# Values kept in SBUF for all tokens, query and key parts written in 4 KB rows, and both attention-stage loops written out

## The reference, cut to what matters

```python
x = x + _layernorm(_L0_attn_ref(_layernorm(x), qkv_w, qkv_b, out_w, out_b))
# _L0_attn_ref: 16 heads of width 16
qkv = x @ qkv_w.T + qkv_b
scores = einsum('bhqd,bhkd->bhqk', q, k) / sqrt(16)
out = einsum('bhqk,bhkd->bhqd', softmax(scores), v)
return out @ out_w.T + out_b
```

## Time and profile before

| | us |
|---|---|
| median of 3 runs | 2459.27 |
| lowest, highest | 2456.72, 2468.26 |
| the profiled execution, its own time | 2469.44 |
| its span, first to last instruction | 2467.7 |

### The profile page before, as it was taken

How to read it: one execution, slowest core, us unless ns; L and a number is a source line. 1 busy time by engine, 2 the same in 40 slices (tenths; PEclk the granted TensorE clock), 3 DMA queues, 4 the chain that set the end, 5 groups by cost and what they waited for, 6 DMA issues and landing times. The chain is left out here.

```text
span 2467.7 us, 40737 instructions
## 1 busy us (share of the span) xinstructions
PE 2150.2 (87%) x14580; PEld 1510.8 (61%) x14580; DVE 1582.9 (64%) x2593; ACT 1256.8 (51%) x2510; POOL 667.2 (27%) x483
## 2 busy tenths in 40 slices
PE   7589999989999945885699999999999999588896
PEld 6533333333333314775588888888888888477775
DVE  7478888888888516775354545455454544568876
ACT  3227777777777713443443444344444444355451
POOL 1010000000000003555333343325243434233432
PEclk9859999999999857888699999999999999799998
DMA  7942232222320021112311221303121211200000
GB/s 227 286 103 72 54 96 62 79 72 61 96 62 28 24 89 49 52 42 80 131 52 53 69 63 60 96 28 121 52 70 53 69 53 61 68 26 27 25 25 19
DMA packets 118685, 176.40 MB, mean 71 GB/s; under 512 B 19289, under 2 KB 73697, under 8 KB 114401
## 3 DMA queue, kind: packets, MB, share of 16 engines
q1 hardware_dynamic: 118496, 173.90, 23.6%
HBM read 126.15 MB, written 46.92 MB: 70 GB/s over the span
## 5 line engine op out<-in xcount | busy, mean ns | idle before, releaser
L576 DVE TENSOR_REDUCE att_sb_mx<-att_ps_psM 128x1 f32<-128x1024 f32 x512 | 607.1, 1218 | 122.3 <-PE att_ps_psM L609 119.5
L714 ACT ACTIVATE att_sb_pt<-att_ps_psS 128x512 f32<-128x512 f32 x1024 | 537.1, 603 | 178.7 <-PE att_ps_psS L627 178.6
L609 PE MATMUL att_ps_psM<-stack_sb_k,stack_sb_q 48*128 48x512 f32 x1024 | 413.8, 480 | 26.1 <-PEq L185 22.8
L627 PE MATMUL att_ps_psS<-stack_sb_q,stack_sb_k 50*128 50x512 f32 x1024 | 390.7, 463 | 38.1 <-ACT att_sb_pt L714 23.2
L627 PEld LDWEIGHTS att_ps_psS<-stack_sb_q,stack_sb_k 50*128 50x128 f32 x1024 | 173.2, 191 | 363.5 <-ACT att_sb_pt L714 306.8
L636 PE MATMUL att_ps_psO<-att_sb_pt,stack_sb_v 128*32 128x512 f32 x2048 | 285.3, 630 | 17.1 <-ACT att_sb_osb L707 17.1
L609 PEld LDWEIGHTS att_ps_psM<-stack_sb_k,stack_sb_q 48*128 48x128 f32 x1024 | 175.2, 193 | 54.6 <-issue 24.2
L2329 POOL TENSOR_TENSOR gla_sb_dm<-gla_sb_dm,gla_sb_masked 128x1024 f32<-128x1024 f32 x64 | 159.3, 2510 | 84.8 <-DMA gla_sb_dm<-decay_rows 84.7
L1995 ACT ACTIVATE gla_sb_sg<-gla_ps_psP 128x512 f32<-128x512 f32 x64 | 38.2, 597 | 280.6 <-PE gla_ps_psP L1756 280.6
L2012 ACT ACTIVATE gla_sb_dm<-gla_sb_dm,gla_sb_neg_g 128x128 f32<-128x128 f32 x512 | 156.3, 391 | 5.0 <-POOL gla_sb_dm L2329 5.0
L2211 DVE TENSOR_TENSOR gla_sb_dm<-gla_ps_psA,gla_sb_dm 128x512 f32<-128x512 f32 x128 | 82.2, 684 | 113.1 <-PE gla_ps_psA L1880 112.6
(11 more groups left out here) (251 smaller groups left out, 4952.8 us busy)
## 6 DMA issues: line engine op xcount, KB each, us to landing
gla_sb_dm<-decay_rows SPq DMA_DIRECT2D x32, 1024.0 KB, 5.4
qk_parts<-qkv_sb_part SPq DMA_DIRECT2D x64, 256.0 KB, 4.1
gla_sb_eg<-decay_exp SPq DMA_DIRECT2D x64, 256.0 KB, 6.6
values<-qkv_sb_va SPq DMA_DIRECT2D x32, 256.0 KB, 3.7
stack_sb_q<-qk_parts SPq DMA_DIRECT2D x64, 128.0 KB, 3.4
stack_sb_k<-qk_parts SPq DMA_DIRECT2D x32, 256.0 KB, 4.1
stack_sb_v<-values SPq DMA_DIRECT2D x16, 512.0 KB, 4.3
att_sb_rb<-sums SPq DMA_DIRECT2D x32, 256.0 KB
```

Of the source, the lines that this page charges most:

```text
L576: nc.vector.tensor_reduce(mx[:, qh, 8 * r + c:8 * r + c + 1], psM[:, t % 2, :], AX.X, ALU.max).then_inc(maxima_taken, 1)
L609: mm = pe.matmul(psM[:, t % 2, c * ST:(c + 1) * ST], q[rs, g, qh, j, n * P:(n + 1) * P], k[rs, g, j, c * ST:(c + 1) * ST], start=True, sto ...
L627: pe.matmul(psS[:, ring_slot(pos), :], k[rs, g, j, s * P:(s + 1) * P], q[rs, g, qh, j, :], start=True, stop=True).then_inc(ring_done, 1)
L714: nc.scalar.activation(pt[:, s % (LAG + 2), ORDER[i], :], psS[:, (pos + 1) % 3, :], ACT.Exp, scale=AD ** -0.5).then_inc(ring_taken, 1)
```

## The change

It has five parts. (1) `stacks.v` holds the values of all 32 token tiles, 17 columns per head (a one and 16 values) and 15 zeros after the last head; `va` is a view of it, so DVE writes values where PE reads them, and `values` with its writes and reads is gone. A value product still takes 32 columns as weights: its own 17 and the 15 that follow, which belong to the next head. (2) POOL sets the ones and zeros after the first inverse root, not before it. (3) `qk_parts` has the high and low row of a channel side by side, so that each of the 8 writes moves 64 rows of 4 KB. (4) Keys are loaded in 6 DMAs a block (4 before); the queries' second half of block 0 is loaded in the last super-tile's turn, not in the one before it. (5) All loops of the two phases are written out.

```diff
-        va = m.sb("va", [P, 2, NT, AH, VW])
+        va = stacks.heads
...
+        def over_all(eng, body):
+            for i in range(NST):
+                body(i, i % 2, i == NST - 1)
...
                 if isinstance(i, int) and i == NST - 2:
                     for o in range(2):
                         sp.wait_ge(part_out[o], 16 * 8)
-                        sp.wait_ge(v_out[o], 16 * NG)
                     stacks.load_first(sp, 0, 0, True)
+                if last:
                     stacks.load_second(sp, 0, 0)
...
                     for g in range(2):
-                        sp.dma_start(parts[mt // 2, i, 2 * (mt % 2) + g].rearrange("a c t -> c a t"),
+                        sp.dma_start(parts[mt // 2, i, 2 * (mt % 2) + g],
                                      part[64 * g:64 * g + 64, u, mt, :, :].bitcast(F32)).then_inc(part_out[u], 16)
-                sp.wait_ge(v_taken, 2 * (i + 1))
-                for g in range(NG):
-                    sp.dma_start(v_aug[i, g], va[:, u, :, HG * g:HG * (g + 1), :].rearrange("p n h c -> p n (h c)")
-                                 ).then_inc(v_out[u], 16)
...
-                if pair == 0 and not first(i, 2):
-                    dve.wait_ge(v_out[u], 8 * NG * (i - u))
                 ns = slice(2 * pair, 2 * pair + 2)
-                nc.vector.tensor_tensor(va[:, u, ns, :, 1:AD + 1],
+                nc.vector.tensor_tensor(va[:, NT * i + 2 * pair:NT * i + 2 * pair + 2, :, 1:VC],
...
             minus_half(nc, pool, half, half_set)
-            for u in range(2):
-                nc.gpsimd.memset(va[:, u, :, :, 0:1], 1.0).then_inc(va_set, 1)
-                nc.gpsimd.memset(va[:, u, :, :, AD + 1:VW], 0.0).then_inc(va_set, 1)
             inverse_root(nc, pool, rs, half, ln_step, LN, rs_ready)
             pool.wait_ge(rs_ready, 1)
+            nc.gpsimd.memset(va[:, :, :, 0:1], 1.0).then_inc(va_set, 1)
+            nc.gpsimd.memset(stacks.v[:, :, AH * VC:], 0.0).then_inc(va_set, 1)
+            pool.wait_ge(va_set, 2)
             stacks.minus(nc.gpsimd, 0)
...
-        self.v = m.sb("v", [P, NG, KT, HG * VW])
+        self.v = m.sb("v", [P, TOKENS // P, AH * VC + VW - VC])
+        self.heads = self.v[:, :, 0:AH * VC].rearrange("p n (h c) -> p n h c", c=VC)
...
-        for blk, a, n in runs(K_PART):
-            if fresh and AD * (blk + n) > 32:
+        for blk, a in enumerate(K_PART):
+            if fresh and AD * (blk + 1) > 32:
...
         self.load_queries(sp, b, 1, g, self.second_in[g])
-        sp.dma_start(self.v[:, g, :, :].rearrange("p (s n) c -> p s n c", s=QH),
-                     self.v_aug[b, :, g].rearrange("s p n c -> p s n c")).then_inc(self.second_in[g], 16)
...
         def over_pairs(eng, body):
-            for g in range(NG):
-                body(0, g, False)
-            with eng.Fori(1, BATCH - 1) as b:
+            for b in range(BATCH):
                 for g in range(NG):
-                    body(b, g, False)
-            for g in range(NG):
-                body(BATCH - 1, g, g == NG - 1)
+                    body(b, g, (b, g) == (BATCH - 1, NG - 1))
...
-                    mm = pe.matmul(psO[VW * j:VW * (j + 1), :], v[:, g, s, VW * j:VW * (j + 1)],
+                    h = VC * (HG * g + j)
+                    mm = pe.matmul(psO[VW * j:VW * (j + 1), :], v[:, KT * b + s, h:h + VW],
```

More of the change, by code:

```diff
@@ L44 @@
 HALF_PE = P // 2
+VC = AD + 1
 FF = 4 * D
@@ L198, in sems, with phase_qkv @@
         return [self.sem(f"{name}{k}") for k in range(n)]
-def phase_qkv(nc, x, w_t, bias, bias_cols, ident_d, parts, v_aug, stacks):
+def phase_qkv(nc, x, w_t, bias, bias_cols, ident_d, parts, stacks):
     with ExitStack() as ctx:
@@ L224, in phase_qkv @@
         xhi_ready, xlo_ready = m.sem("xhi_ready"), m.sem("xlo_ready")
-        rs_ready, va_set = m.sem("rs_ready"), m.sem("va_set")
+        rs_ready = m.sem("rs_ready")
         qk_done, v_done, v_taken = m.sem("qk_done"), m.sem("v_done"), m.sem("v_taken")
         hi_ready, lo_ready = m.sem("hi_ready"), m.sem("lo_ready")
-        part_out, v_out = m.sems("part_out", 2), m.sems("v_out", 2)
+        va_set, part_out = m.sem("va_set"), m.sems("part_out", 2)
         xv = tokens(x)
@@ L255, in body @@
                     for g in range(2):
-                        sp.dma_start(parts[mt // 2, i, 2 * (mt % 2) + g].rearrange("a c t -> c a t"),
+                        sp.dma_start(parts[mt // 2, i, 2 * (mt % 2) + g],
                                      part[64 * g:64 * g + 64, u, mt, :, :].bitcast(F32)).then_inc(part_out[u], 16)
-                sp.wait_ge(v_taken, 2 * (i + 1))
-                for g in range(NG):
-                    sp.dma_start(v_aug[i, g], va[:, u, :, HG * g:HG * (g + 1), :].rearrange("p n h c -> p n (h c)")
-                                 ).then_inc(v_out[u], 16)
-            over_supertiles(sp, body)
+            over_all(sp, body)
             for s in part_out:
                 sp.wait_ge(s, 16 * 8 * NST // 2)
-            for s in v_out:
-                sp.wait_ge(s, 16 * NG * NST // 2)
         @block.vector
@@ L310, in _ @@
             dve.wait_ge(b_ready, 32)
-            dve.wait_ge(va_set, 4)
+            dve.wait_ge(va_set, 2)
             def body(i, u, last):
@@ L325, in body @@
                     take_values(i, u, pair)
-            over_supertiles(dve, body)
+            over_all(dve, body)
         @block.tensor
@@ L362, in body @@
                         mm.then_inc(v_done, 1)
-            over_supertiles(pe, body)
+            over_all(pe, body)
         @block.scalar
@@ L386, in body @@
                     take_turned(i + 1, 1 - u)
-            over_supertiles(act, body)
+            over_all(act, body)
         @block.gpsimd
@@ L403, in body, with __init__ @@
                     inverse_root(nc, pool, rs, half, ln_step, LN * (i + 2), rs_ready)
-            over_supertiles(pool, body)
+            over_all(pool, body)
 class Stacks:
-    def __init__(self, m, parts, v_aug):
-        self.parts = parts.rearrange("t (b s) g a c x -> t b s g a c x", s=QH)
-        self.v_aug = v_aug.rearrange("(b s) g p n c -> b s g p n c", s=QH)
+    def __init__(self, m, parts):
+        self.parts = parts.rearrange("t (b s) g c a x -> t b s g c a x", s=QH)
         self.q = m.sb("q", [P, NG, QH, 2, ST], F32R)
         self.k = m.sb("k", [P, NG, 2, SEQ], F32R)
-        self.v = m.sb("v", [P, NG, KT, HG * VW])
+        self.v = m.sb("v", [P, TOKENS // P, AH * VC + VW - VC])
+        self.heads = self.v[:, :, 0:AH * VC].rearrange("p n (h c) -> p n h c", c=VC)
         self.minus_set, self.first_in, self.second_in = m.sems("minus_set", NG), m.sems("first_in", NG), m.sems("second_in", NG)
-    FIRST = 16 * 2 * (len(runs(Q_PART)) + len(runs(K_PART)))
-    SECOND = 16 * (2 * len(runs(Q_PART)) + 1)
+    FIRST = 16 * 2 * (len(runs(Q_PART)) + len(K_PART))
+    SECOND = 16 * 2 * len(runs(Q_PART))
     def minus(self, eng, g):
@@ L429, in load_queries @@
                 sp.dma_start(self.q[HALF_PE * r + AD * blk:HALF_PE * r + AD * (blk + n), g, qh, :, :].bitcast(F32),
-                             self.parts[0, b, qh, g, a:a + n].rearrange("a (c j r) t -> r (a c) j t", r=2, j=2)[r]
+                             self.parts[0, b, qh, g, :, a:a + n].rearrange("(c j r) a t -> r a c j t", r=2, j=2)[r]
                              ).then_inc(sem, 16)
@@ L2405, in scratch @@
         return nc.dram_tensor(name, shape, dt, kind="Internal").ap()
-    parts = scratch("qk_parts", [2, NST, NG, 2, HG * AD, ST])
-    v_aug = scratch("values", [NST, NG, P, NT, HG * VW])
+    parts = scratch("qk_parts", [2, NST, NG, HG * AD, 2, ST])
     dens, att_t = scratch("sums", [QH, HG * ST]), scratch("attended", [NST, NG * P, ST])
@@ L2413, in sandwich @@
     with ExitStack() as ctx:
-        stacks = Stacks(Place(nc, ctx, "stack"), parts, v_aug)
-        phase_qkv(nc, x, qkv_w_t, qkv_b, qkv_b_cols, ident, parts, v_aug, stacks)
+        stacks = Stacks(Place(nc, ctx, "stack"), parts)
+        phase_qkv(nc, x, qkv_w_t, qkv_b, qkv_b_cols, ident, parts, stacks)
         phase_attention(nc, stacks, ident, dens, att_t)
```

4 lines of the change are left out of this document (2 added, 2 removed).

## The result

The changed kernel took 2531.32 us (median of 4 runs, 2522.94 to 2534.50), the kernel before 2457.99 beside it. The ratio is 1.0285, 95% interval 1.0246 to 1.0325: 73 us slower, where 31.6 us faster was forecast. The profiled execution took 2534.5, its span is 2532.7.

What follows compares the result with a forecast made beforehand. phase_qkv was taken as bound by PE for three super-tiles, then by SP's queue and DMA engines together. Gains of 27.5 us at its end and 4.1 at the attention loop's jump took 2459.3 to 2427.7 us, range 2412 to 2444.

Steps and rivals of the forecast that it cites:

- Pace of phase_qkv: Without writes of values, super-tiles keep PE's pace of 9.57 us to the end, instead of slowing to 12.52.
- T0: Start of the first super-tile's first ACT copy in phase_qkv; predicted 20.1 us, after +0.9 us for POOL's new memsets.
- End of phase_qkv: SP's last writes end sooner, so phase_attention starts at 100.3 instead of 127.8: 27.5 us less, bounds 21.9 to 29.7.
- The attention loop written out: At the loop's jump in phase_attention, a unit takes 21.95 us instead of 26.09: 4.1 us less.
- Loads in phase_attention: 14 issues a block for 13, 512 KB less, DMA share 0.29, blocks loaded units ahead: cost taken as 0.
- Value products: In phase_attention, same count and 32 columns from other start addresses: cost 0, groups of four staying at 630 ns.
- the rival: Value products get slower from new weight addresses: 10% costs 31.7 us, 20% gives 2492 us; chance 0.05.
- the 7.5: Rival that PE's clock stays up or returns early in phase_attention: 7.5 us less, 2420 us; chance 0.13.
- The DMA side: Rival that DMA still limits phase_qkv, at worst 12.52 us a super-tile, giving 2439.5 us; chance 0.11.
- code fetch: Rival that written-out code arrives late, stalling PE 3.02 us in each of 16 units: 2476 us; chance 0.04.
- The 4 KB rows: Part writes in phase_qkv, priced by byte like 2 KB rows; cover if dearer 0.7 us a super-tile, 9%.
- The sum: Whole kernel: 27.5 + 4.1 = 31.6 us less, from a median of 2459.3 to 2427.7 us; chance 0.67.

Runs made afterwards that it cites:

- e1_single: The changed kernel with each query block loaded by itself instead of two stacked blocks in one load: 2433.15 us, 0.9891 of the kernel before.
- e9_nopad: e5_values_only with keys loaded block by block, 6 DMAs instead of 4: 2430.32 us, 0.9885 of the kernel before.
- e3_loops_only: The kernel before with both loops written out and nothing else changed: 2455.89 us, 0.9992 of the kernel before.
- e5_values_only: The changed kernel with the kernel before's parts layout, parts writes, query and key loads; values stay in SBUF, loops written out: 2425.64 us, 0.9876.
- e4_first_only: The changed kernel with first-half queries loaded block by block, second-half queries still as a stacked pair: 2442.07 us, 0.9914 of the kernel before.
- e10_spread: The changed kernel with load_second issued a unit later than load_first: 2446.67 us, 0.9954 of the kernel before.

## Why the prediction was wrong, by its steps

- **Pace of phase_qkv: right.** 9.57 was said, 9.58 measured, T0 20.16 for 20.1. T0 to T1 took 10.68, 1.1 more; why, no run tells.
- **End of phase_qkv: direction right, size off.** The term was 27.5 us, bounds 21.9 to 29.7; the trace has 18.2. Two errors. The last writes end 5.2 us later than said. Of this 2.5 us are there before the first of the 30 issues: SP ends the sixth super-tile's writes at 77.57 (71.05 + 6.52), where I had it free at 75.1. The 30 issues take 23.8 us for 21.1, and 2.0 of these 2.7 lie in the last eight, 0.95 us each (7.60 / 8) where I took 0.70. And 3.8 + 0.3 us of drain became 8.3, since four loads of the pair stand in the queue ahead of them: in e1_single, which has none, it is 3.9 (the last write issued at 103.24, the start at 107.12). The first matmul of phase_attention in the change, e1_single and e9_nopad:

```profile
109.65 1.23 PE L603 MATMUL att_ps_psM<-stack_sb_k,stack_sb_q 48*128 48x512 f32 x4 [14.36 <-PEq L186]
```

```profile
107.12 1.22 PE L603 MATMUL att_ps_psM<-stack_sb_k,stack_sb_q 48*128 48x512 f32 x4 [11.99 <-PEq L186]
```

```profile
105.19 1.23 PE L603 MATMUL att_ps_psM<-stack_sb_k,stack_sb_q 48*128 48x512 f32 x4 [10.97 <-PEq L186]
```

  So 20.7 and 22.6 us are gained here where the loads are spread.
- **The attention loop written out: right in size** (4.1 in e3_loops_only's trace), too small for the times.
- **Loads in phase_attention: the step that failed.** "That is the cover, and I take 0" counted issues and KB against a mean DMA share of 0.29. Both counts were right. The new access pattern was not looked at: `(a c)` became `a c`, and in the order of SP the 32 partitions of its other side still look like before. What the cover had to hide was 512 KB a block on two engines; at the 50 GB/s of 228 to 236 us that is some 10 us (an estimate), and the mean share of sixteen engines says nothing about it. Measured: 98.2 us for the load of the pair where I took 0, of which by the traces 82 are in the long units and 8.3 before the copy of unit 0, 2.5 of those in the late start.
- **Value products: right.** The page's row after gives

```profile
L631 PE MATMUL att_ps_psO<-att_sb_pt,stack_sb_v 128*32 128x512 f32 x2048 | 303.2, 667 | 17.0 <-ACT att_sb_osb L702 17.0
```

  and looks like the rival, 667 for 630 in the earlier trace rows. It isn't: in e9_nopad, with the same columns and no long units, it is

```profile
L631 PE MATMUL att_ps_psO<-att_sb_pt,stack_sb_v 128*32 128x512 f32 x2048 | 275.3, 609 | 17.3 <-ACT att_sb_osb L702 17.3
```

  From 206 to 236 us, at a granted clock of 1.00, the median is 592 ns in the change and 593 in e9_nopad. The 667 is half clock after the gaps, an effect and no cause.
- **The rivals.** None was the case. The clock is 0.50 from 109.65 to 157.00 in the change; from the phase's start to the copy of unit 0 it takes 62.1 us before and in e9_nopad, and 59.1 in e5_values_only, where the clock rises between 140 and 150 us: at most 3 of the 7.5. The DMA side did not hold the pace at 12.52. Of the slower side I named value products and code fetch; both were tested and aren't it. The 4 KB rows I had priced per byte, with a doubt about their speed alone.
- **The sum.** With the failed step mended, e1_single takes 2433.15, e9_nopad 2430.32 and e5_values_only 2425.64 us, for 2427.7 predicted. That they come so near is in part luck. In the traces of the kernel before and of e5_values_only the last copy of `osb` comes 45.1 us sooner: 26.8 before the copy of unit 0 and 4.1 at the jump, which is my sum, but another 14.4 in the last two intervals (26.19 and 27.79 for 21.96 and 17.57), where the clock fell in one and not in the other. No term of mine holds that. It is likely also the 10.2 us by which the profiled execution before stands above its median.

## What to carry to other kernels

When a layout changes, write down the outermost dimension of both sides of every DMA that goes with it, not its bytes, its packets or its number: a pair that no longer merges into one stride can take 14 of 16 DMA engines from a transfer. Then ask what small load is queued behind it and which engine's in-order stream waits for that; its slack, here between two and four such loads, decides whether every second unit is 22.0 us long or 26 to 32. A DMA share near 2/16 with an engine waiting for a DMA is how it looks in the windows, and small packets that don't grow by 16 with each DMA is how it looks in the counts. Here a split by the dimension that is 2 took it away (2433.15 us); loads spread over units took most of it (2446.67).

## What the runs showed of the hardware that was not expected

In the last two units of phase_attention the granted clock falls in 7 of the 12 traces and holds in 5. In the kernel before it falls at 845 us, and from 838 to 846 no idle time of PE is over 0.45 us. Windows of the kernel before and of e5_values_only, each the 83 us before the last copy of `osb`:

```profile
801.00:840.00 39.00, 35.90 (x222) 13.46 (x222) 31.75 (x29) 30.85 (x62) 2.75 (x6) 1.00 0.05 16
840.00:884.00 44.00, 40.75 (x147) 10.47 (x146) 0.25 (x1) 23.08 (x45) 2.54 (x2) 0.56 0.09 31
```

```profile
756.00:795.00 39.00, 35.83 (x229) 13.61 (x228) 33.62 (x31) 30.56 (x62) 3.46 (x6) 1.00 0.09 29
795.00:839.00 44.00, 37.51 (x219) 11.77 (x223) 10.51 (x11) 34.49 (x68) 2.99 (x4) 1.00 0.10 32
```

The last interval between copies of `osb` is 27.8 us with the fall (27.5 in the change) and 17.6 without. That is 10 us for the same work, nearly the 12.3 that I took for the limit of the measurement. It is likely part of why the executions of e4_first_only and e10_spread lie 25 and 19 us apart; one trace each can't show it. What decides it stays open.
